# Cross-attention and expert network on one core: pairs of images with row-tiled scores, and every step placed by a time relative to its pair or chunk

## What is computed

```python
x = x + xattn(layernorm(x), ctx, ...)      # below, per image b
  q = (xn @ q_w + q_b) as 16 heads of 8;  k, v = (ctx @ kv_w + kv_b) as 16 heads of 8
  attn = softmax(q * 8**-0.5 @ k.T)        # 128 x 77 for each head
  out = (attn @ v) @ proj_w + proj_b
x = x + ffn(layernorm(x), ...)
  xn = layernorm(x) * gamma + beta
  probs = softmax(xn @ router_w.T / 1.5);  w, idx = top_k(probs, 2)
  out = sum over the two experts of w_e * (silu(xn @ W1[e]) @ W2[e]) + x
```

## Time and profile before

| | us |
|---|---|
| Median of 3 runs | 843.11 (839.19 to 843.46) |
| The profiled execution, own time | 845.43 |
| its span from first to last instruction | 843.5 |
| PE, DVE, ACT, POOL busy | 721.3, 543.0, 499.3, 492.0 |
| first score, first expert matmul | 33.8, 514.7 |
| mean granted clock of PE | 0.926 of full |

### The profile page before, as it was taken

How to read it: one execution, slowest core, us unless ns; L and a number is a source line. 1 busy time by engine, 2 the same in 40 slices (tenths; PEclk the granted TensorE clock), 3 DMA queues, 4 the chain that set the end, 5 groups by cost and what they waited for, 6 DMA issues and landing times. The chain is left out here.

```text
span 843.5 us, 16697 instructions
## 1 busy us (share of the span) xinstructions
PE 721.3 (86%) x5164; PEld 496.7 (59%) x5164; DVE 543.0 (64%) x1857; ACT 499.3 (59%) x1037; POOL 492.0 (58%) x692
## 2 busy tenths in 40 slices
PE   1699999998989899998999977988899889999960
PEld 1455556555656555564665545766677677777840
DVE  1456666765776667675666734666677777688972
ACT  1366666565566566564666544856675766677840
POOL 5422526657566747665765560664577777765772
PEclk9699989988999989998999965989999999999995
DMA  5455454554565537455442434655987875779964
GB/s 180 110 115 135 113 135 115 161 122 130 118 159 145 139 81 186 101 158 121 105 105 67 100 107 167 202 192 192 318 301 241 290 214 185 254 246 366 377 214 179
DMA packets 152287, 146.49 MB, mean 174 GB/s; under 512 B 53403, under 2 KB 108584, under 8 KB 152040
## 3 DMA queue, kind: packets, MB, share of 16 engines
q1 hardware_dynamic: 140808, 121.57, 50.0%
q0 software_dynamic: 9088, 19.68, 6.8%
q10 hardware_dynamic: 2304, 4.20, 1.3%
HBM read 81.56 MB, written 40.86 MB: 145 GB/s over the span
## 5 line engine op out<-in xcount | busy, mean ns | idle before, releaser
L837 ACT ACTIVATE P<-pt 77x512 f32<-77x512 f32 x256 | 151.5, 593 | 117.3 <-PE pt L641 108.8
L1350 POOL DMA_INDIRECT ys<-yo,to x156 | 167.6, 1074 | 75.2 <-issue 39.6
L1343 POOL DMA_INDIRECT xs<-zz,idx x128 | 131.1, 1024 | 94.8 <-PE pt L563 35.3
L973 DVE TENSOR_REDUCE mx<-ps 128x4 f32<-128x308 f32 x256 | 118.8, 471 | 88.4 <-PE ps L628 84.3
L1213 DVE TENSOR_TENSOR sl<-sf,sh 128x512 fp32r<-128x512 f32 x156 | 107.2, 691 | 63.6 <-ACT sh L884 28.3
L641 PE MATMUL pt<-qd,kc 128*77 128x512 f32 x256 | 115.2, 451 | 15.6 <-DMA qd<-nm 14.9
L652 PE MATMUL po<-P,v 77*9 77x128 f32 x2048 | 107.2, 284 | 4.8 <-ACT osb L845 4.5
L628 PE MATMUL ps<-kd,qc 128*128 128x308 f32 x256 | 107.5, 421 | 1.6 <-DMA kd<-kc 0.9
L882 ACT ACTIVATE sf<-ps 128x512 f32<-128x512 f32 x78 | 46.9, 601 | 68.8 <-PE ps L563 46.6
L641 PEld LDWEIGHTS pt<-qd,kc 128*77 128x77 f32 x256 | 38.9, 152 | 50.5 <-issue 29.1
L628 PEld LDWEIGHTS ps<-kd,qc 128*128 128x128 f32 x256 | 50.6, 198 | 25.9 <-issue 19.9
(11 more groups left out here) (207 smaller groups left out, 1802.7 us busy)
## 6 DMA issues: line engine op xcount, KB each, us to landing
qd<-qc SPq DMA_DIRECT2D x128, 128.0 KB
ws<-wsd SPq DMA_DIRECT2D x26, 512.0 KB
w1o<-wsd SPq DMA_DIRECT2D x26, 512.0 KB
w2o<-wsd SPq DMA_DIRECT2D x26, 512.0 KB
xb<-xs SPq DMA_DIRECT2D x39, 288.0 KB
kd<-kc SPq DMA_DIRECT2D x128, 77.0 KB
wsd<-ws SPq DMA_DIRECT2D x8, 1024.0 KB
y<-ys SPq DMA_DIRECT2D x32, 256.0 KB
```

The source lines that it names most:

```text
L837: eng.activation(P[k % 4][:, :], pT[k % 2][0:CS, :], ACT.Exp, scale=SCALE).then_inc(sems["p"], 1)
L973: eng.tensor_reduce(mx[b % 2][:, 4 * g:4 * g + 4], ps[k % 2][:, 0:KC].rearrange("p (j m) -> p j m", j=4), AX.X, ALU.max, negate=True).then ...
L1343: eng.indirect_dma_start(out=xs, out_offset=at, in_=zz[b][:, j % 4, :], in_offset=None).then_inc(sems[f"sw{b}"], 16)
L1350: eng.indirect_dma_start(out=ys, out_offset=at, in_=yo[u % NYO][:, q, :], in_offset=None).then_inc(sems[f"ys{u % NYO}"], 16)
```

## The change

The steps of the attention phase now work on **pairs** of images p, and three things are rebuilt.

- **Scores by row tiles.** `kd` and `qd` are gone with their transfers and their clearing. `SC(p, i, h)` makes the scores of image i of the pair for the half h, that is for j = 2h and 2h+1 of all four groups: eight matmuls that use 32 rows each (128 x 78 columns), alternating between two row tiles of the array and between the two banks of `ps`. `ST(p, i, h)` does the same transposed (77 x 128 each) into the two banks of `pT`. So both tiles are now written as a whole and are no longer double-buffered: the next half waits until DVE has taken the maxima (of 2 x 4 x 77 columns in one instruction), or ACT the exp (77 x 1024, step `EX`).
- **Pairs.** One transpose of 32 rows of maxima, one copy, and one transfer (`ND`) straight into row 24 of each 32 in `qc`; `v18` holds both images' v in different columns, so that one accumulation of 32 matmuls leaves both images in one bank `po`, with one copy (`OE`), four transposes, one reciprocal, one product (256 columns), one copy, and one addition for the pair.
- **Order.** Each step has a time in a table, relative to its pair (10.0 apart) or chunk (20.0 apart); all are sorted by it.

Smaller edits: ACT copies all four `QG` groups (DVE did two); `XP` moved from POOL to DVE as one instruction; `xin` has 6 buffers, not 4; the first 16 blocks, not 18, take rows of the chunks 0 to 11, and the table of blocks is made one chunk earlier. The expert blocks' own steps are the same.

```diff
-K1 = 18
+K1 = 16
...
+PERIOD = 10.0
+PAIR = dict(SC00=-2.2, SC01=1.1, SC10=2.7, SC11=4.4, MT=7.0, ND=7.1, ST00=9.8, EX00=9.9, ST01=12.2, EX01=12.3, ST10=13.5, EX10=14.0,
+            ST11=15.8, EX11=16.1, PV=18.7, OE=18.7, OT=21.8, ON=24.2, PR=25.9)
+CHUNK = dict(LX=-67.5, A0=-36.8, CT=-36.8, A1=-33.6, A2=-32.5, XH=-32.4, XP=-30.6, XT=-28.4, KP=-21.7, KL=-20.6, QP=-19.6, QL=-18.5,
...
+SCATTER, SCATTER_GAP, LAYER = 66.0, 2.0, 0.8
...
+    timed = [(PERIOD * p + t, named(name, p)) for p in range(NP) for name, t in PAIR.items()]
+    timed += [(2 * PERIOD * c + t, named(name, c)) for c in range(NC) for name, t in CHUNK.items()]
+    end = PERIOD * (NP - 1) + PAIR["PR"]
...
+    timed.sort(key=lambda it: it[0])
+    out = [step for t, step in timed if t <= end]
...
-COUNTED = (7, 11, 12, 15)
+COUNTED = (7, 10, 11, 15)
...
-        kc = tile(sa, "kc", [128, 4, 4, CS], R, 2)
-        qd = tile(sa, "qd", [128, 2, 4, 4, S], R, 2)
-        kd = tile(sa, "kd", [128, 2, 4, 4, CS], R, 2)
-        v9 = tile(sa, "v9", [CS, 4 * H, 9], F, 2)
-        P = tile(sa, "P", [CS, 4 * S], F, 4)
-        mx = tile(sa, "mx", [128, 16], F, 2)
-        nm = tile(sa, "nm", [16, 128], R, 2)
+        kc = tile(sa, "kc", [128, 4, 4, CE], R, 2)
+        v18 = tile(sa, "v18", [CS, 2, 2, H, 18], F, 2)
+        P = tile(sa, "P", [CS, 4, 4, S], F, 4)
+        mx = tile(sa, "mx", [128, 32], F, 2)
+        nm = tile(sa, "nm", [32, 128], R, 2)
...
-        pm, ps, pT, po = pt("pm", 3), pt("ps", 2), pt("pt", 2), pt("po", 1)[0]
+        pm, po = pt("pm", 3), pt("po", 1)[0]
+        pT = st.enter_context(nc.psum_tensor("pt", [128, 2, 512], F))
+        ps = st.enter_context(nc.psum_tensor("ps", [128, 2, 512], F))
...
-            def KD(p):
-                c, i, s = p // 2, 2 * (p % 2), p % 2
-                for g in range(4):
-                    w.wait_ge(*kc_done(c, g))
-                w.wait_ge("c_kd", s + 1)
-                if p >= 2:
-                    w.wait_ge("S", 8 * (p - 1))
-                for j in range(4):
-                    load(kd[s][32 * j:32 * j + 32, :, :, j, :].rearrange("p i g m -> p (i g) m").bitcast(F),
-                         kc[c % 2][32 * j:32 * j + 32, i:i + 2, :, :].rearrange("p i g m -> p (i g) m").bitcast(F), f"kd{s}")
...
+            def ND(p):
+                c, i = p // 2, 2 * (p % 2)
+                w.wait_ge(*freed("MT", p))
+                load(qc[c % 2][24:128:32, i:i + 2, :, :].rearrange("p i g n -> p (i g) n").bitcast(F),
+                     nm[p % 2][:, :].bitcast(F), f"nm{p % 2}")
...
-                        w.wait_ge(f"sw{s}", 128 * ((NC - 2 - s) // 2 if u < K1 else NC // 2))
+                        w.wait_ge(f"sw{s}", 128 * ((NC - 3 - s) // 2 if u < K1 else NC // 2))
...
+            def SC(p, i, h):
+                c, n_ = p // 2, 2 * (p % 2) + i
+                for g in range(4):
+                    w.wait_ge(*qc_done(c, g))
+                    w.wait_ge(*kc_done(c, g))
+                w.wait_ge("c_kc", 2)
+                w.wait_ge("mx", 4 * p + 2 * i + h)
+                for g in range(4):
+                    for j in (2 * h, 2 * h + 1):
+                        at_j = slice(32 * j, 32 * j + 32)
+                        ins = eng.matmul(ps[:, j % 2, g * CE:(g + 1) * CE], qc[c % 2][at_j, n_, g, :], kc[c % 2][at_j, n_, g, :],
+                                         start=True, stop=True)
+                ins.then_inc(sems["S"], 1)
...
+            def ST(p, i, h):
+                c, n_ = p // 2, 2 * (p % 2) + i
+                w.wait_ge(f"nm{p % 2}", 16 * (p // 2 + 1))
+                w.wait_ge("p", 4 * p + 2 * i + h)
+                for g in range(4):
+                    for j in (2 * h, 2 * h + 1):
+                        at_j = slice(32 * j, 32 * j + 32)
+                        ins = eng.matmul(pT[0:CS, j % 2, g * S:(g + 1) * S], kc[c % 2][at_j, n_, g, 0:CS], qc[c % 2][at_j, n_, g, :],
+                                         start=True, stop=True)
+                ins.then_inc(sems["T"], 1)
...
+                for g in range(4):
+                    for i in range(2):
+                        for j in range(4):
+                            ins = eng.matmul(po[32 * j:32 * j + 18, g * 128:(g + 1) * 128], v18[c % 2][:, p % 2, i, 4 * g + j, :],
+                                             P[(2 * p + i) % 4][:, j, g, :], start=(i == 0), stop=(i == 1))
...
+            def EX(p, i, h):
+                w.wait_ge("T", 4 * p + 2 * i + h + 1)
+                w.wait_ge("Og", p - 1)
+                two = slice(2 * h, 2 * h + 2)
+                eng.activation(P[(2 * p + i) % 4][:, two, :, :], pT[0:CS, :, :].rearrange("m j (g n) -> m j g n", g=4), ACT.Exp,
+                               scale=SCALE).then_inc(sems["p"], 1)
...
+            def XP(c):
+                w.wait_ge("ld_v", N_LDV)
+                w.wait_ge("xh", 4 * c + 4)
+                eng.tensor_tensor(xin[c % NX][:, :, :], xin[c % NX][:, :, :], pbb[:, :].unsqueeze(1).to_broadcast([128, 4, 128]),
+                                  ALU.add).then_inc(sems["xp"], 1)
```

415 lines of the change are left out of this document (152 added, 263 removed).

## The result

The changed kernel takes **981.7 us** (median of 4 runs, 969.8 to 988.2) against 843.1 before. The ratio of the faster executions (969.8 and 977.9) to those of the kernel before is 1.156, 95% interval 1.146 to 1.166, so 16% slower. The profiled execution took 969.8 us, its span 968.0. Forecast were 765, and 728 to 815 as range: wrong in sign.

The account below looks back on a forecast made before the run. PE was taken to bound the attention phase: 11.4 us work plus 0.6 waits, 12.0 per pair. First score 34.5, 31 pairs 372, then 26 and 3.7 gave 436, 78.5 us less; blocks 0; median 765, range 728 to 815.

Parts of the forecast that it names:

- the rival with chance 0.09: Attention phase: waits at tiled pieces put a third of it at 1.2 GHz, 15.8 us a pair, 883 us; chance 0.09.
- for all waits and low clock together: Attention phase: 0.6 us a pair added to PE's work for every wait and low-clock stretch.
- PE bounds the phase: Attention phase: PE sets the time per pair, busy 92% before; the other engines have 5 us to spare.
- A half of the scores 0.65: PE, row-tiled scores: eight loads and short matmuls take 0.65 us, between 0.55 side by side and 1.0 serial.
- Transposed 0.5: PE, row-tiled transposed scores: a half takes 0.5 us, between ends of 0.43 and 0.66.
- Product 2.0: PE, product with v for a pair: 64 records in one block take 2.0 us instead of 2.7.
- 11.4 us a pair: Attention phase: PE's work per pair after the change, against 12.3 before; low ends 10.7, high ends 13.4.
- Exp hidden but for 0.3 a pair: Transposed scores without double buffer: waiting for the exp costs PE about 0.3 us per pair on average.
- The transfer of the maxima is hidden: Attention phase: 4.0 us of PE work covers the maxima's transfer, with 0.8 to spare; most of 12.1 us waits go.
- Most of the low clock: Attention phase: most low-clock time goes together with most of the 12.1 us of waits for the maxima's transfer.
- First expert matmul 436: End of the attention phase: the first expert matmul starts at 436 us instead of 514.7, 78.5 less.
- 0 in the blocks: Expert blocks: nothing changed in them, so a gain of 0; the loss in their first eighth stays.

Follow-up runs that it names:

- both sides undone: Changed kernel with scores and transposed scores both full matmuls over 128 rows (308 and 512 columns), pairs and order kept: 819.2 us, ratio 0.972 to the kernel before.
- stand-alone streams: PE alone, the reference's computation left out, some 40 us of each kind of matmul without waits, behind full matmuls; clock 0.50 in some kinds, 1.00 in others.
- the stand-alone run: PE alone, the reference's computation left out, ten attention pairs of the changed kernel's mixture without waits: 10.1 us a pair, clock 0.93 or more.

## Why the prediction was wrong

**The failed step is the dismissal of the clock**, the rival with chance 0.09: "Against it: the single waits are 0.3 us, not 3." In the sum it is the 0.6 us a pair "for all waits and low clock together": a pair took 18.4 us, some 6.6 more than its work at the full clock. The waits were indeed small, smaller than said (about 1 us in 290), and the clock fell all the same, twice with no wait recorded ahead of it. The argument took an idle PE for the only thing that lowers the clock, since in the trace of before nearly all low stretches stood behind idle times. The rule of the Trainium skill ("TensorE: Matmul & The Clock Gate", HAM oscillation — how this bites in real kernels) is likewise to avoid idle gaps of PE; by it the changed kernel should have kept the full clock. Rows differ from it: 238 of 239 us busy, granted 0.50. The rival's own condition was met several times over: it decided from 22% of PE's work at the low level, and with a mean clock of 0.60 in 110 to 400 us four fifths of the time and two thirds of the work went there. Its price, 883, was too low for that reason: it took a third. Its mechanism named the right part ("tiled pieces, in which only a part of the array works") and leant on waits that weren't there.

Point by point:
- **PE bounds the phase**: right, before and after (288 of 290 us busy).
- **A half of the scores 0.65**: 0.57 at the full clock. **Transposed 0.5**: 0.42. **Product 2.0**: 1.87. Row tiles do run side by side, near the low ends. **11.4 us a pair** of work, **12.0** with waits: in the three stretches at the full clock PE is busy 57.3 of 60 us for 156 score records, which is 11.8 of work and 12.3 with waits. At 12.3 throughout, the time would have been some 9 us over the forecast (31 pairs of 0.3), about 774 and inside the range.
- **Maximum 0.79, exp 1.04**: 0.799 and 1.018. **Exp hidden but for 0.3 a pair**: 0.7 us in 290; a slower PE hides more.
- **The transfer of the maxima is hidden**: right, no wait for it is left; with both sides undone and room for one pair in `qd` it costs 17.3 us in 290.
- **"Most of the low clock" goes with that wait**: the false link. The low clock grew.
- **First score 34.5**: 35.3. **First expert matmul 436**: 654. The 218 us are 6.4 us a pair (18.4 against 12.0) on 32 pairs, 205, and a tail at the low clock.
- **0 in the blocks**: 15 us fewer there (314 against 329). The kernel with both sides undone has 315 as well, with the scores undone 321, so most of this comes with what these kernels share, the pairs and the new order; which of the two was not tested. I had counted it as nothing.

What the forecast described is nearly the kernel with the scores alone undone: 12.3 us a pair, first expert matmul at 458, 771.9 us. The row tiles of one side are in it, and they gave what they promised.

**What is shown, and what stays open.** Shown: the loss is the clock, not work and not waits; with full score matmuls (308 columns) or full transposed ones (512) in place of the row tiles, or with both, the clock stays at 0.92 or more (three kernels, two of them in several executions); scores in matmuls of 78 columns over all rows lower it as row tiles do (0.52), so the rows are not its cause as such; some stand-alone streams run at half the clock with PE busy all the time. Not shown: why the kernel's mixture stays at half the clock while the same mixture in the stand-alone run keeps the full one. Short waits move it in that direction, but the kernel's clock also falls without them and stays low without them. Whether the numbers that the array multiplies have a part is unclear too: the twins with superfluous matmuls could not be told apart. And that it is thinness which counts is a reading of the streams; the kernel with 256 columns moved speaks against its simplest form.

## What to carry to other kernels

A PE that is busy 99% can still run at half speed, here for 239 us on end: read the granted clock beside the busy share, and when a change makes matmuls thinner (row tiles, few columns against a long load), take its saving as at risk until the clock row is seen. Bring such tiles in on one side first and measure each side alone: here each gained, and the two together lost 16%. A rival that names the right part of the kernel should not be set aside because its usual cause is missing.

## What the hardware showed unexpectedly

- Half the clock for 239 us on end with PE busy 238 of them, and falls of the clock with no wait recorded in the 6 us ahead.
- Row tiles run side by side, in proportion to their number. With 128 columns loaded and 78 moved, at half the clock, one row tile of 32 rows takes 0.212 us a matmul (62 us for 292 in the stream), two take 0.106 (41 us for 388) and four 0.054 (29 us for 534). A matmul over all 128 rows takes 0.213 (61 us for 287), as one tile does.
- In two row tiles 128 columns moved cost no more than 78: 0.106 us at half the clock (47 us for 444). 256 columns cost 0.060 at the full clock (21 us for 348). In the kernel a piece of 8 with 78 columns takes 0.57 us at the full clock, 0.071 a matmul, with the change of mode in it.
- Changing between row-tiled and full matmuls costs time as well. In the stand-alone mixture, with 8 superfluous matmuls of 0.23 us (37 us for 161 in the stream of 512 columns), pairs with no low slice in them take 13.4 and 14.1 us in turn, against 10.1 and 10.2 without. That is 1.7 us more in the mean than the matmuls themselves. By the order of the pieces they add 5 changes of mode (between row tiles, column tiles and the whole array) in one pair and 9 in the next, so some 0.25 us for each, an estimate.
- Executions of one row-tiled kernel on one chip differ by 6% (963 to 1,023 us, the changed kernel) to 11% (875 to 973 us, with 8 superfluous matmuls of the queries), where those of the kernel before agree within 2%: where the clock wavers, so does the time.
